# A four-layer modulated 1-D convolution: a new order of GpSimd's work, of the opening and of the edge samples

## The reference

```python
s = style @ mw.T + mb
weight = SCALE * w * s[:, None, :, None]
demod = rsqrt(sum(weight * weight, axis=(2, 3)) + EPS)
weight = weight * demod[:, :, None, None]
...
if typ == 'same':       out = conv_same(x, weight) + b
elif typ == 'upsample': out = blur(conv_up(x, weight) + b, 2.0 * blur_k, (1, 1))
else:                   out = conv_down(blur(x, blur_k, (2, 2)), weight) + b
...
x = x + layers(x, cond_512, ...)
```

## Time and profile before

| what | value |
|---|---|
| median of 3 runs (lowest, highest) | 905.13 us (903.54, 907.57) |
| the profiled execution, its own time | 902.8 us |
| its span, first to last instruction | 901.0 us |
| TensorE matmul busy | 730.2 us (81%) |
| VectorE / ScalarE / GpSimd busy | 468.3 / 311.4 / 396.7 us |
| share of the chain that ended last: TensorE, "issue" | 72%, 16% |
| mean granted clock of TensorE | 0.851 |

### The profile page before, as it was taken

How to read it: one execution, slowest core, us unless ns; L and a number is a source line. 1 busy time by engine, 2 the same in 40 slices (tenths; PEclk the granted TensorE clock), 3 DMA queues, 4 the chain that set the end, 5 groups by cost and what they waited for, 6 DMA issues and landing times.

```text
span 901.0 us, 12263 instructions
## 1 busy us (share of the span) xinstructions
PE 730.2 (81%) x4434; PEld 665.0 (74%) x4434; DVE 468.3 (52%) x711; ACT 311.4 (35%) x501; POOL 396.7 (44%) x520
## 2 busy tenths in 40 slices
PE   5495977789887888988877987788997777987796
PEld 4485866679777777877777877777886677876796
DVE  6956833475553455456555444347555345544462
ACT  4321422343332334333234424233333234423342
POOL 3551634525444544354454344453444454344430
PEclk9786978888888889888889888888888888888899
DMA  5123346764456665455666445666444666445865
GB/s 188 39 75 64 107 108 149 158 141 104 112 120 158 158 159 105 123 121 128 159 159 131 111 112 125 156 159 158 99 120 100 157 158 148 99 114 115 205 154 138
DMA packets 130091, 116.97 MB, mean 130 GB/s; under 512 B 6064, under 2 KB 96560, under 8 KB 130032
## 3 DMA queue, kind: packets, MB, share of 16 engines
q1 hardware_dynamic: 129376, 114.62, 54.2%
q10 hardware_dynamic: 656, 1.57, 0.5%
HBM read 36.47 MB, written 33.55 MB: 78 GB/s over the span
## 4 chain that ended last, share of the span: by engine, by line
PE 72%; issue 16%; DVE 8%; DMA 1%; ACT 1%; POOL 1%; ACTq 0%; DVEq 0%; SPq 0%; POOLq 0%
PE po L170 14%; PE po L171 13%; PE po L172 13%; PE pg L170 6%; PE pg L171 6%; PE pg L172 6%; PE pg L175 3%; PE pg L176 3%; PE pm L172 2%; PE pm L171 2%; PE pm L170 2%; PE pe L371 1%; DVE Gf L701 1%; DVE T L679 1%; DMA A2f<-in_a 1%
## 5 line engine op out<-in xcount | busy, mean ns | idle before, releaser
L170 PE MATMUL po<-xh,W 128*128 128x256 f32 (+1 forms) x640 | 246.6, 385 | 132.7 <-issue 119.8
L170 PEld LDWEIGHTS po<-xh,W 128*128 128x128 f32 x640 | 140.1, 219 | 152.9 <-issue 137.8
L171 PE MATMUL po<-xl,W 128*128 128x256 f32 (+1 forms) x640 | 240.2, 375 | 0.0
L172 PE MATMUL po<-xh,W 128*128 128x256 f32 (+1 forms) x640 | 238.3, 372 | 0.0
L705 DVE TENSOR_TENSOR Wf<-pg,S 128x512 f32<-128x512 f32 x64 | 44.2, 691 | 262.4 <-PE pg L172 242.8
L172 PEld LDWEIGHTS po<-xh,W 128*128 128x128 f32 x640 | 139.3, 218 | 18.7
L171 PEld LDWEIGHTS po<-xl,W 128*128 128x128 f32 x640 | 140.4, 219 | 15.1
L462 ACT ACTIVATE T<-po,cv,DD 128x512 f32<-128x512 f32 x64 | 49.7, 776 | 252.4 <-PE po L172 252.4
L582 POOL TENSOR_TENSOR Q3l<-Q3f,Q3h 128x256 fp32r<-128x256 f32 x31 | 26.1, 841 | 177.3 <-ACT Q3h L469 177.3
L670 DVE TENSOR_TENSOR xl<-X,xh 128x1032 fp32r<-128x1032 f32 x64 | 96.3, 1504 | 2.0 <-ACT xh L438 2.0
L590 POOL TENSOR_TENSOR Q2l<-Q2f,Q2h 128x512 fp32r<-128x512 f32 x31 | 71.2, 2297 | 54.8 <-ACT Q2h L477 54.8
(11 more groups left out here) (175 smaller groups left out, 1602.0 us busy)
## 6 DMA issues: line engine op xcount, KB each, us to landing
X<-in_xin SPq DMA_DIRECT2D x64, 516.0 KB, 6.0
out<-T SPq DMA_DIRECT2D x64, 512.0 KB, 3.6
W<-W SPq DMA_DIRECT2D x96, 256.0 KB, 6.7
W<-W SPq DMA_DIRECT2D x32, 384.0 KB, 7.9
V<-V SPq DMA_DIRECT2D x32, 128.0 KB, 6.8
V<-W SPq DMA_DIRECT2D x32, 64.0 KB, 5.4
V<-Vx SPq DMA_DIRECT2D x32, 64.0 KB, 5.1
E<-in_ed ACTq DMA_DIRECT2D x1, 768.0 KB, 7.7
```

Source lines behind the costliest of these rows:

```text
L170: eng.matmul(o, wh_, rh, start=first, stop=False)
L171: eng.matmul(o, wh_, rl, start=False, stop=False)
L172: return eng.matmul(o, wl_, rh, start=False, stop=last)
```

## The change

- **GpSimd.** `finish(2g-1)` goes to the first step of a group, ahead of `q3_full`; `finish(2g)` to the third step, ahead of the low of unit (g+2, 2). `q3_full` moves to the first step, `x_parts(2g+3)` to the third, behind that low. The lows of (1, 2) and (1, 3) stand ahead of the loop.
- **SyncE.** `load(2g+5)` is written at the end of group g, no longer at the head of group g+1.
- **Opening.** Units (1, 2) and (1, 3) join `PROLOGUE`, the table `FIRST` goes, so that units (1, 4) to (1, 6) stand at step 1 and no more at step 2. The second constant product comes behind `conv(0)`.
- **Edges.** The first 32 samples are chunks of 8 (steps 0 to 3) and 24 (steps 4 to 7). TensorE's edge part for step b is now issued in step b+1, between its units and its `conv`.

```diff
+CHUNKS = [(0, 8), (8, 24), (32, 32), (64, 32), (96, 32)]
...
-PROLOGUE = [(0, 0), (0, 1), (0, 2), (0, 3), (1, 0), (1, 1), (0, 4), (0, 5), (0, 6)]
-FIRST = [[(1, 2), (1, 3)], [(2, 0), (2, 1)], [(1, 4), (1, 5), (1, 6)], [(2, 2), (2, 3)]]
+PROLOGUE = [(0, 0), (0, 1), (0, 2), (0, 3), (1, 0), (1, 1), (0, 4), (0, 5), (0, 6), (1, 2), (1, 3)]
 SLOTS = [[(2, 0), (2, 1)], [(1, 4), (1, 5), (1, 6)], [(2, 2)], [(2, 3)]]
...
             edge_at[(0, k)] = (0, k)
-        for c in range(1, B // EC):
-            for k in range(4):
-                edge_at[(EC // NG * c - 5 + k, 2)] = (c, k)
+            edge_at[(1, k)] = (1, k)
+            for c in range(2, len(CHUNKS)):
+                edge_at[(CHUNKS[c][0] // NG - 5 + k, 2)] = (c, k)
...
+            load(XR)
             for g in range(NGR):
                 n = NG // Q * g
-                if n + XR < NQ:
-                    load(n + XR)
                 if n:
                     store(n - 1)
                 if n + 1 + XR < NQ:
...
                 store(n)
+                if n + 2 + XR < NQ:
+                    load(n + 2 + XR)
...
-            for x in PROLOGUE[6:9]:
+            for x in PROLOGUE[6:11]:
                 unit(*x)
...
+            constant(2, 1, SC_K2)
             for b in range(B):
                 for x in units_of(b):
                     unit(*x)
+                if b and divmod(b - 1, NG) in edge_at:
+                    edge(*edge_at[divmod(b - 1, NG)])
                 conv(b)
-                if divmod(b, NG) in edge_at:
-                    edge(*edge_at[divmod(b, NG)])
+                if b == 0:
+                    constant(3, 3, SC_K3)
...
             for b in range(B):
                 g, i = divmod(b, NG)
                 if i == 0 and g + 1 < NGR:
                     identity(g + 1)
+                if i == 2 and g:
+                    finish(b // Q - 1)
                 for x in units_of(b):
                     if x[1] < 4:
                         low(*x)
-                if i == 1 and g + 3 < NGR:
+                if i == 0 and g == 1:
+                    finish(0)
+                if i == 0 and g:
+                    finish(b // Q - 1)
+                if i == 0 and g + 3 < NGR:
                     q3_full(g + 3)
-                if i == 1 and g + 1 < NGR:
-                    x_parts(b // Q + 3)
                 if i == 1 and g + 3 < NGR:
                     q3_low(g + 3)
-                if b % Q == 1 and b > Q:
-                    finish(b // Q - 1)
+                if i == 2 and g + 1 < NGR:
+                    x_parts(b // Q + 2)
```

More of the change, by code:

```diff
@@ L37, in units_of @@
     g, i = divmod(b, NG)
-    return [(g + d, u) for d, u in (SLOTS if g else FIRST)[i] if g + d < NGR]
+    return [(g + d, u) for d, u in SLOTS[i] if g + d < NGR]
 ORDER = PROLOGUE + [x for b in range(B) for x in units_of(b)]
@@ L408, in _, with constant @@
             pe.wait_ge(s_cl, 1)
-            for x in PROLOGUE[6:9]:
+            for x in PROLOGUE[6:11]:
                 unit(*x)
-            for l, k, at in ((2, 1, SC_K2), (3, 3, SC_K3)):
+            def constant(l, k, at):
                 pe.wait_ge(s_sc, at)
@@ L532, in _ @@
             q3_high(2)
+            high(1, 2)
+            high(1, 3)
             for b in range(B):
@@ L634, in _ @@
             q3_low(2)
+            low(1, 2)
+            low(1, 3)
             for b in range(B):
@@ L738, in edge @@
+                y1, y2 = Y1[:, 0:n], Y2[:, 0:n]
                 dve.wait_ge(s_e, 4 * c + k + 1)
                 if k == 0:
[L740 to L743, removed]
+                    v = y1[:, :, 0:7]
+                    link(tt(v, got(0, 7), bc(b0z[:, cs], 7), ALU.add))
+                    tt(ZE[lo, 0:n, 1:8], v[lo], bc(D10[lo, cs], 7), ALU.mult)
+                    tt(ZE[hi, 0:n, 0:7], v[hi], bc(D10[hi, cs], 7), ALU.mult).then_inc(s_ed, 1)
@@ L744, in edge @@
                 elif k == 1:
[L745 to L749, removed]
+                    tt(y1[:, :, 0:7], got(0, 7), bc(S[:, 1, cs], 7), ALU.mult)
+                    link(tt(y1[:, :, 7:13], got(7, 6), bc(S[:, 1, cs], 6), ALU.mult))
@@ L753, in edge @@
                     link(m)
-                    link(tt(Y1[:, :, 0:13], Y[:, :, 1:14], Y[:, :, 0:13], ALU.add))
-                    link(tt(Y2[:, :, 0:12], Y1[:, :, 1:13], Y1[:, :, 0:12], ALU.add))
-                    link(tt(Y1[:, :, 0:11], Y2[:, :, 1:12], Y2[:, :, 0:11], ALU.add))
+                    link(tt(y1[:, :, 0:13], Y[:, 0:n, 1:14], Y[:, 0:n, 0:13], ALU.add))
+                    link(tt(y2[:, :, 0:12], y1[:, :, 1:13], y1[:, :, 0:12], ALU.add))
+                    link(tt(y1[:, :, 0:11], y2[:, :, 1:12], y2[:, :, 0:11], ALU.add))
@@ L757, in edge @@
                     for h, o in ((lo, 1), (hi, 0)):
-                        m = dve.scalar_tensor_tensor(out=U[h, :, o:o + 11], in0=Y1[h, :, 0:11], scalar=0.25,
+                        m = dve.scalar_tensor_tensor(out=U[h, 0:n, o:o + 11], in0=y1[h, :, 0:11], scalar=0.25,
                                                      in1=bc(S[h, 2, cs], 11), op0=ALU.mult, op1=ALU.mult)
@@ L761, in edge @@
                 elif k == 2:
-                    v = Y1[:, :, 0:10]
-                    link(tt(v, pe_[:, 0:10 * EC].rearrange("p (b n) -> p b n", n=10), bc(DD[:, 2, cs], 10), ALU.mult))
+                    v = y1[:, :, 0:10]
+                    link(tt(v, got(0, 10), bc(DD[:, 2, cs], 10), ALU.mult))
                     for h, o in ((lo, 2), (hi, 0)):
-                        m = dve.tensor_scalar(HH[h, :, o:o + 10], v[h], BB[h, 0, 2:3], None, ALU.add)
+                        m = dve.tensor_scalar(HH[h, 0:n, o:o + 10], v[h], BB[h, 0, 2:3], None, ALU.add)
                     link(m)
[L767 to L770, removed]
+                    link(tt(y1[:, :, 0:11], HH[:, 0:n, 1:12], HH[:, 0:n, 0:11], ALU.add))
+                    link(tt(y2[:, :, 0:10], y1[:, :, 1:11], y1[:, :, 0:10], ALU.add))
+                    link(tt(y1[:, :, 0:9], y2[:, :, 1:10], y2[:, :, 0:9], ALU.add))
+                    dve.scalar_tensor_tensor(out=XB[:, 0:n], in0=y1[:, :, 0:9], scalar=0.125, in1=bc(S[:, 3, cs], 9),
                                              op0=ALU.mult, op1=ALU.mult).then_inc(s_ed, 1)
                 else:
-                    v = Y1[:, :, 0:4]
-                    link(tt(v, pe_[:, 0:4 * EC].rearrange("p (b n) -> p b n", n=4), bc(DD[:, 3, cs], 4), ALU.mult))
-                    for h, n, x in ((lo, 0, 1), (hi, 2, 4)):
+                    v = y1[:, :, 0:4]
+                    link(tt(v, got(0, 4), bc(DD[:, 3, cs], 4), ALU.mult))
+                    for h, q, x in ((lo, 0, 1), (hi, 2, 4)):
                         for r, d in ((0, lo), (1, hi)):
                             m = dve.scalar_tensor_tensor(
-                                out=EP[d, cs, n:n + 2], in0=v[h, :, r:r + 3:2], scalar=BB[h, 0, 3:4],
+                                out=EP[d, cs, q:q + 2], in0=v[h, :, r:r + 3:2], scalar=BB[h, 0, 3:4],
                                 in1=XE[h, cs, x + r:x + r + 3:2], op0=ALU.add, op1=ALU.add)
@@ L874, in _ @@
             sums_low(0)
+            full(1, 2)
+            full(1, 3)
             dve.wait_ge(s_pp, 5)
@@ L905, in _ @@
                     edge(c, k)
-                    if k == 3 and c + 1 < B // EC:
+                    if k == 3 and c + 1 < len(CHUNKS):
                         edge_in(c + 1)
```

29 lines of the change are left out of this document (17 added, 12 removed).

## The result

| | before | after |
|---|---|---|
| median of 4 runs (lowest, highest) | 905.44 us (903.54, 907.57) | 700.29 us (697.92, 700.94) |
| span of the profiled execution | 901.0 us | 696.1 us |
| TensorE matmul busy | 730.2 us (81%) | 665.7 us (96%) |
| mean granted clock | 0.851 | 0.988 |

The ratio is 0.7729, with a 95% interval from 0.7704 to 0.7754: 22.7% less time. The forecast was 710 us with a range of 690 to 795. The profiled execution of the changed kernel is its shortest; the other three span 698.4 to 699.1 us.

The account below looks back on a forecast made before the run. Late copies of W, behind a store waiting for GpSimd's `finish`, stall each group's first convolution and slow the clock. 901.0 - 174 - 19 - 2 = 706 us span, 708 with 1.8 outside; predicted 710 us, range 690 to 795.

Parts of the forecast that it names:

- Rival B: At the first convolutions, the stall doesn't move at all, as W's low parts decide the copies' landing: 884 us; chance 0.06.
- T: In each group, the start of its first convolution, conv(4g), without a stall; the forecast counts times from it.
- The sum of the steady part: Groups 2 to 28: 27 x 19.5 = 526.5, plus 16.2, plus 10, is 553 in place of 726.7 us: -174 us.
- my 16.2: Over groups 2 to 28, the edge parts of three chunks add 16.2 us.
- the 10 us for stalls in six groups with edge parts: Steady part: 2.7 us for each of three groups (k = 1), 0.7 for each of the three next longest.
- the T + 20.9 that I gave: Group with edge part k = 1: copies of W land at T + 20.9, 1.4 us late, plus up to 1.35 for clock.
- 100 forecast for conv(8): Opening: conv(4) comes at about 74, conv(8) 26 us later, at 100 in place of 118.7.
- The -19 us of the opening: Opening: conv(8) at 100 in place of 118.7 us saves 19 us, with bounds of 0 and 27.
- rival D: The opening yields nothing while the steady part does: 729 us; chance 0.06.
- The end: Groups 29 and 30: -1.3 for a full-clock start, -0.8 for line 724 as `x_parts` comes later: -2 us.
- Rival A: A stall of, say, 2 us remains in every group, with or without slow clock: 764 to 826 us; chance 0.2.
- Rival C: Slower by the clock: without pauses TensorE might be granted 1.2 GHz for long, kernel 1140 us; chance 0.03.

Follow-up runs that it names:

- pair held: The changed kernel, with SyncE holding the odd pair's store and the load behind it until the first low part of W is written: 746.63 us, ratio 0.8269.

## Why the prediction was right, and where it was off

- **What bounds the kernel: right.** The first convolution of a group waited for the copies of W, and the copies for a store whose `finish` stood behind `q3_low`. Moving that call alone (709 us), moving it back (885) and putting the copies first (706) all agree, and with the copies first the late call costs nothing (696). Rival B, a stall that stays, is out with them.
- **The single clean hand-over in the trace of before was a sound model.** From group 29 I had the store at T + 4.9, the first copy at T + 8.8 and the last landing at T + 17.2 to 17.5; the changed kernel shows T + 5.1, T + 8.8 and T + 17.1. Counting from the first copy (17.2) was the closer way; counting from the store, 12.6 us, gave 0.4 too much here and 0.8 with the pair held.
- **The sum of the steady part: 553 forecast, 539.2 measured.** A plain group takes 19.45 us for my 19.5, and edge parts add 14.0 us for my 16.2. The term that failed was the 10 us for stalls in six groups with edge parts. The copies of group 13 did land late, at 336.72 + 8.7 = 345.4, T + 20.75, close to the T + 20.9 that I gave. But I set that against T + 19.5. The group has the next edge part on TensorE in it and lasts 21.07 us, so conv(56) began at 345.74, 0.3 us after the landing. I had counted that part's time in the sum and left it out of the deadline. With 0.3 us to spare, that no group stalls was close. The rows of group 13 (T = 324.67): its store, its last copy with that copy's landing, and the first convolution of group 14.

```profile
332.55 0.38 SPq L217 DMA_DIRECT2D out<-T  x1
...
336.72 1.25 SPq L227 DMA_DIRECT2D W<-W  x1
...
W<-W SPq DMA_DIRECT2D x1, 256.0 KB, 8.7
...
345.74 0.40 PE L171 MATMUL po<-xh,W 128*128 128x512 f32 x1
```

- **The opening: 100 forecast for conv(8), 103.76 measured.** conv(0) began at 47.66 (forecast 47.6) and conv(4) at 77.0 (forecast 74); the second group took 26.76 us for 26. VectorE's chain for 8 samples was no shorter than 5.1 us, and GpSimd's instructions stretched it.
- **The -19 us of the opening were put down to the wrong part.** Conv(8) came 15.0 us earlier. But the 118.74 that I compared with holds an 8.24 us stall of the hand-over, which two things remove, each by itself: the moved call (0.83 us is left of it) and the rest of the change with the call put back (nothing is left). With the steady part mended and the old opening, the runs are at 709.5 and 706.2 us. So the opening and the edges together add 6 to 9 us to the moved call, not 19, and rival D (729 us with an opening that yields nothing) was mispriced. The new opening also depends on the later place of TensorE's edge parts: in the run without it the first two groups take 75.1 us, 14.5 more than with the old opening. The split in 8 and 24 costs 1.6 to 3.6 us.
- **The end: -2 forecast.** From conv(116) to the last instruction it was 55.5 us and is 53.1. Line 724 (740 now) takes 0.56 us in group 30, where it took 1.34 beside `x_parts`.
- **Rival A** had a stall of 2 us in every group at 764 us and more. It did not come, by a margin of some 2 us in most groups. The run with the pair held has it: 1.2 us a group, and 747 us. **Rival C** fell: the clock is 1.00 for the 539 us without a pause.

## What to carry to other kernels

On a queue that takes its entries in order, a transfer whose wait ends late holds back all that stands behind it, however idle the engines and the DMA are: put a transfer that an engine waits for ahead of those that nobody waits for, or make sure that the wait in front of it ends early. When a stall is weighed against a deadline, put everything of that stretch that the waiting engine has to do into the deadline too. Where the trace of a periodic kernel has one period in which the suspected wait is missing, such as the last ones of the loop, it can serve as the model of what all periods will be, as it did here to 0.4 us.

## What the runs showed of the hardware

- A stall of 2.9 to 8.2 us at each hand-over brought TensorE's matmuls to the 1.2 GHz level behind it, 65.7 us over 27 groups. With the pair held, stalls of up to 2.2 us left the clock at 1.00 over 21 hand-overs on end. Between 2.3 and 3.7 us it went either way: the clock fell with the stalls of 2.30 and 2.71 us (pair held) and with each one from 2.92 us up in the kernel before, and did not with 2.63 (before), 2.76 (pair held), 3.02 and 3.65 (call put back). No run here shows what decides between them.
- The upper level of the clock record read 0.95 in the trace of before and 1.00 in the traces of all other kernels here, although a first convolution took 3.52 us in both kernels. The 0.95 was no slower clock for the matmuls, and the means 0.851 and 0.988 differ in part by that reading alone: the call put back, with the same stalls, reads 0.89 over groups 2 to 28 where before reads 0.85.
- A VectorE instruction on 48 to 56 elements took 0.92 to 1.16 us beside GpSimd's 1.1 us instructions, and 0.25 us without; the same on 192 to 224 elements took 0.31 to 0.34 us with GpSimd idle.
